# Query and exponentials moved to a PSUM bank, and the projected query to the feed-forward output's bank, in a graph attention kernel

## What is computed

```python
# layers 0 and 1, l = 0, 1 (h = relu(layernorm(x)) @ w_in + b_in at first)
xn = layernorm(h, ln1_g[l], ln1_b[l])
q, k, v = xn @ wq[l] + bq[l], xn @ wk[l] + bk[l], xn @ wv[l] + bv[l]
scores = einsum('ehd,ehd->eh', q[dst], k[src]) * scale
ex = exp(scores - segment_max(scores, dst)[dst])
attn = ex / segment_sum(ex, dst)[dst]
agg = segment_sum(attn * v[src], dst)
h = h + agg @ wo[l] + bo[l]
h = h + gelu(layernorm(h, ln2_g[l], ln2_b[l]) @ w1[l] + b1[l]) @ w2[l] + b2[l]
# layer 2, after x = x + h and h = relu(layernorm(x)): keys K[src] + 0.2 * rel_w[edge_type],
# no feed-forward part; x = x + layernorm(agg @ Wo + bo + h) * gamma + beta
```

## Time and profile before

| | |
|---|---|
| median of 3 runs | 5768.97 us (5768.95 to 5776.74) |
| the profiled execution: its own time | 5769.38 us |
| its span | 5767.4 us, 100749 instructions |
| mean granted clock of TensorE, share of full speed | 0.81 |
| PE busy | 3774.7 us (65%) |
| DVE busy | 3920.1 us (68%) |
| ACT busy | 1907.6 us (33%) |
| POOL busy | 3630.9 us (63%) |
| layer 0, layer 1, layer 2 begin on DVE at | 926.5, 2490.6, 4061.9 us |

### The profile page before, as it was taken

How to read it: one execution, slowest core, us unless ns; L and a number is a source line. 1 busy time by engine, 2 the same in 40 slices (tenths; PEclk the granted TensorE clock), 3 DMA queues, 4 the chain that set the end, 5 groups by cost and what they waited for, 6 DMA issues and landing times. The chain is left out here.

```text
span 5767.4 us, 100749 instructions
## 1 busy us (share of the span) xinstructions
PE 3774.7 (65%) x17126; PEld 2738.3 (47%) x17127; DVE 3920.1 (68%) x6783; ACT 1907.6 (33%) x4023; POOL 3630.9 (63%) x3068
## 2 busy tenths in 40 slices
PE   2056663677778888836777787878456665555555
PEld 2023332455556666525555565656344444444443
DVE  9533333777777777547777777765588888777766
ACT  5023331233334444413333344444222333232333
POOL 0422225788887776457888877753588777666643
PEclk9987776888889999968888899999666666666666
DMA  5022224566556655346666666553455555454442
GB/s 182 1 67 93 93 93 129 164 188 185 180 174 211 199 181 178 109 141 180 197 194 184 191 208 195 181 166 108 128 167 170 161 154 151 143 149 129 132 116 70
DMA packets 361804, 870.94 MB, mean 151 GB/s; under 512 B 142032, under 2 KB 154813, under 8 KB 361748
## 3 DMA queue, kind: packets, MB, share of 16 engines
q0 software_dynamic: 243088, 718.69, 42.4%
q1 hardware_dynamic: 111604, 119.56, 6.5%
q10 hardware_dynamic: 7056, 32.12, 1.4%
HBM read 791.89 MB, written 149.65 MB: 163 GB/s over the span
## 5 line engine op out<-in xcount | busy, mean ns | idle before, releaser
L1036 POOL DMA_INDIRECT kv<-kv_dram,idx x2616 | 3177.7, 1215 | 1232.0 <-issue 753.2
L1492 PE MATMUL ps_acc<-kv,ident 128*128 x5232 | 1430.0, 441 | 206.8 <-DVE kv L1176 205.6
L1492 PEld LDWEIGHTS ps_acc<-kv,ident 128*128 128x128 f32 x5232 | 1168.6, 227 | 491.2 <-issue 287.6
L1098 DVE TENSOR_TENSOR kv<-kv,rec_in (+1 forms) x654 | 790.1, 1220 | 379.4 <-DMA kv<-kv_dram,idx 243.1
L1103 DVE TENSOR_REDUCE sc<-kv 128x32 f32 (+2 forms) x654 | 785.7, 1211 | 13.6 <-DVE kv L1098 12.9
L1176 DVE TENSOR_TENSOR kv<-kv,ex x654 | 756.9, 1220 | 22.1 <-issue 10.6
L1486 PE MATMUL ps_acc<-acc_scaled,ident 128*128 128x256 f32 x306 | 145.9, 569 | 690.9 <-DVE zrun L1168 690.9
L1337 ACT COPY acc<-ps_acc 128x256 f32<-128x256 f32 x153 | 57.0, 372 | 1504.1 <-PE ps_acc L1495 1504.1
L1540 PE MATMUL ps_big<-xnaT,w_ffn 128*128 128x128 f32 x3136 | 376.4, 278 | 135.3 <-ACT xnaT L1394 135.3
L1540 PEld LDWEIGHTS ps_big<-xnaT,w_ffn 128*128 128x128 f32 x3136 | 359.1, 192 | 157.5 <-ACT xnaT L1394 80.1
L1486 PEld LDWEIGHTS ps_acc<-acc_scaled,ident 128*128 128x128 f32 x306 | 60.5, 247 | 743.9 <-DVE zrun L1168 743.9
(11 more groups left out here) (207 smaller groups left out, 5182.9 us busy)
## 6 DMA issues: line engine op xcount, KB each, us to landing
rec_in<-rec_dram SPq DMA_DIRECT2D x147, 512.0 KB, 4.8
rec_dram<-rec_out POOLq DMA_DIRECT2D x98, 512.0 KB, 3.3
kv<-kv_dram,idx POOLq DMA_INDIRECT x2616, 3.8
rec_dram<-rec_in ACTq DMA_DIRECT2D x49, 640.0 KB
windows<-kv SPq DMA_DIRECT2D x46, 408.0 KB, 2.6
rec_in<-rec_dram SPq DMA_DIRECT2D x49, 128.0 KB, 5.4
w_ffn<-in_L_gnn_w SPq DMA_DIRECT2D x4, 1024.0 KB, 6.5
meta<-slot_meta SPq DMA_DIRECT2D x153, 24.0 KB, 3.1
```

Source lines behind the costliest of these rows:

```text
L1036: pool.indirect_dma_start(kv[:, u * W + slot, :], None, kv_dram[l], bass.IndirectOffsetOnAxis(ap=idx[:, u, slot:slot + 1], axis=0), bounds ...
L1098: nc.vector.tensor_tensor(at, at, q, ALU.mult).then_inc(s["mul"], 1)
L1492: mm = nc.tensor.matmul(ps_acc[:, 0:D], ident[:], at[:, :, slot, :].rearrange("p a d -> p (a d)"), start=False, stop=False, skip_group_che ...
```

## The change

The SBUF tile `ex` is gone. The bank `ps_q` now belongs to ACT and DVE alone: its columns 0 to 255 (`ps_query`) hold the query of the block being scored, columns 256 on (`exw`) the exponentials. ACT copies the query from `rec_in` to `ps_query` (`query_row`), for block b+1 within the exp of block b's last round, between the wait for `to_exp` and the exp itself; DVE's `start` waits for this copy (`query`) instead of the record's load. DVE's products read `ps_query`, its weightings and `rescale` read `exw`.

The projected query of a finished block, which had been in `ps_q`, goes to columns 0 to 255 of `ps_w`, whose other half holds the feed-forward output. PE makes it in a step of its own (`next_q`), behind the earlier rounds and after DVE has read the feed-forward output of block b-2 (`second`), and `feed_out` waits for the record of the block before to be copied out (`recq`). In layer 2 the transposed types, the pairs and the products use `ps_kv` and `ps_w` without `ps_q`; the third group of pairs waits for ACT's first `away`. ACT's last block is written out apart from its loop in all layers.

```diff
@@ -182,7 +182,6 @@
-        ex = sb("ex", [P, (W + 1) * 8])
@@ -216,9 +215,10 @@
-        ps_types = ps_q[0:W, 0:P // 2].bitcast(BF16)
-        ps_pairs = [ps_w[:], ps_q[:], ps_kv]
-        ps_rel = [ps_big[:, 0, :], ps_big[:, 1, :], ps_w[:]]
+        ps_query = ps_q[:, 0:D]
+        ps_types = ps_kv[0:W, 0:P // 2].bitcast(BF16)
+        ps_pairs = [ps_w[:], ps_kv, ps_w[:]]
+        ps_rel = [ps_big[:, 0, :], ps_big[:, 1, :], ps_kv]
@@ -597,10 +597,13 @@
-        def project_qkv(l, ofT, done):
-
-            project(ps_kv, ofT, w_qkv[l], B_QKV + 3 * l * D, (0, 2 * D))
-            project(ps_q[:, 0:D], ofT, w_qkv[l], B_QKV + 3 * l * D, (2 * D, 3 * D)).then_inc(done, 1)
+        def project_kv(l, ofT):
+
+            return project(ps_kv, ofT, w_qkv[l], B_QKV + 3 * l * D, (0, 2 * D))
+
+        def project_q(to, l, ofT):
+
+            return project(to, ofT, w_qkv[l], B_QKV + 3 * l * D, (2 * D, 3 * D))
@@ -911,7 +915,7 @@
-            exw = ex[:, 0:(W + 1) * H]
+            exw = ps_q[:, D:D + (W + 1) * H]
@@ -1074,7 +1077,7 @@
-                        q = flat(rec_in[:, one(b % RING), AT_Q:AT_Q + D]).unsqueeze(1).broadcast_to([P, CH, D])
+                        q = ps_query.unsqueeze(1).broadcast_to([P, CH, D])
@@ -1179,7 +1182,8 @@
-                        dve.wait_ge(s["rec"], by_rec * (b + 1))
+                        dve.wait_ge(s["query"], b + 1)
+                        settle(dve)
@@ -1187,7 +1191,7 @@
-                            step(nc.vector.tensor_tensor(prod[:], flat(r[:, :, AT_Q:AT_Q + D]), flat(r[:, :, AT_K:AT_K + D]), ALU.mult))
+                            step(nc.vector.tensor_tensor(prod[:], flat(r[:, :, AT_K:AT_K + D]), ps_query, ALU.mult))
@@ -1345,8 +1349,16 @@
-                    def exp_round(k):
+                    def query_row(b):
+                        act.wait_ge(s["rec"], by_rec * (b + 1))
+                        settle(act)
+                        nc.scalar.copy(ps_query, flat(rec_in[:, one(b % RING), AT_Q:AT_Q + D])).then_inc(s["query"], 1)
+
+                    def exp_round(k, upcoming=None):
                         act.wait_ge(s["to_exp"], k + 1)
+                        if upcoming is not None:
+                            settle(act)
+                            query_row(upcoming)
                         nc.scalar.activation(exw, smw, ACT.Exp, scale=scale).then_inc(s["exped"], 1)
@@ -1434,7 +1446,7 @@
-                        nc.scalar.copy(flat(to[:, :, 2 * D:3 * D]), ps_q[:, 0:D]).then_inc(s["recq"], 1)
+                        nc.scalar.copy(flat(to[:, :, 2 * D:3 * D]), ps_w[:, 0:D]).then_inc(s["recq"], 1)
@@ -1458,7 +1470,7 @@
-                            exp_round(k)
+                            exp_round(k, None if last_block(b) else b + 1)
@@ -1477,7 +1489,8 @@
-                    iterate(act, iteration)
+                    query_row(0)
+                    iterate(act, iteration, whole=NB - 1)
@@ -1497,12 +1510,15 @@
+                        if not isinstance(k, int):
+                            pe.wait_ge(s["relrow"], GROUPS * k)
+                            settle(pe)
                         pe.wait_ge(s["types"], k + 1)
                         nc.tensor.transpose(ps_types, types[:], ident_b[:]).then_inc(s["typesT"], 1)
-                        if not isinstance(k, int):
-                            pe.wait_ge(s["relrow"], GROUPS * k)
                         pe.wait_ge(s["typesTs"], k + 1)
                         for g in range(GROUPS):
+                            if g == 2:
+                                pe.wait_ge(s["away"], k * GROUPS + 1)
@@ -1544,6 +1560,9 @@
                         to = ps_w[:, D:2 * D]
+                        if not isinstance(b, int) or b >= 2:
+                            pe.wait_ge(s["recq"], b - 1)
+                            settle(pe)
                         bias(to, B_2 + l * D)
@@ -1554,12 +1573,18 @@
-                    def next_qkv(b):
+                    def next_kv(b):
...
-                        project_qkv(l + 1, xnbT, s["qkv"])
+                        project_kv(l + 1, xnbT)
+
+                    def next_q(b):
+                        if not isinstance(b, int) or b + 1 < NB:
+                            pe.wait_ge(s["second"], 2 * b + 3)
+                            settle(pe)
+                        project_q(ps_w[:, 0:D], l + 1, xnbT).then_inc(s["qkv"], 1)
@@ -1590,6 +1615,9 @@
+                        if exists(b - 3) and not typed:
+                            next_q(b - 3)
+                        if exists(b):
                             sums(k, chunk0, filled)
```

More of the change, by code:

```diff
@@ L874, in iteration @@
                             settle(pe)
-                        project_qkv(0, xnbT, p_qkv)
+                        project_kv(0, xnbT)
+                        project_q(ps_q[:, 0:D], 0, xnbT).then_inc(p_qkv, 1)
                 iteration(0)
@@ L894, in build @@
             "norm", "residual", "second", "scale1", "scale2", "aggT", "aggTs", "w", "var1", "sd1", "var2", "sd2", "rs1", "xn1", "xT1", "xTs1", "f1", "g", "f2", "rs2", "xn2", "xT2", "xTs2", "qkv", "recq", "types", "typesT", "typesTs", "pairs", "away", "onehot", "relp", "relrow", "outx", "mixed", "last",
-            "used", "taken")}
+            "used", "taken", "query")}
         numbers = sorted(handle.num for handle in between.values())
@@ L920, in last_round, with iterate @@
                 return (round_number(rounds_before + earlier), chunks_before + earlier * CPS, last)
-            def iterate(eng, iteration, peeled=DEPTH):
-                whole = NB - 1 if typed else NB
+            def iterate(eng, iteration, peeled=DEPTH, whole=NB - 1 if typed else NB):
                 for b in range(peeled):
@@ L1580, in iteration @@
                         if exists(b - 3) and not typed:
-                            next_qkv(b - 3)
+                            next_kv(b - 3)
                         if exists(b):
```

## The result

The changed kernel takes 5797.8 us (median of 6 runs, 5795.6 to 5799.1) beside 5773.7 us for the kernel before (6 runs, 5769.0 to 5786.9): the ratio is 1.0038, 95% interval 1.0026 to 1.0051. It is slower by 0.4%, where 5748 us was forecast. That lies inside the stated range of 5700 to 5805 us, but on the other side of the kernel before. The profiled execution has a span of 5795.9 us, 28.5 more than before.

A forecast was written before the change was run, and what follows sets the result against it. POOL was taken to bound blocks of five, DVE and its waits blocks of four. Gains of 44, 19, 26 and 24 us against costs of 83 and 9 gave -21, so 5748 us from 5769.4; range 5700 to 5805.

The forecast's parts named there:

- What bounds the kernel: Layers 0 and 1: POOL bounds blocks of five; DVE and its feed-forward waits, 1.2 and 1.1 us, bound blocks of four.
- The gathers: POOL: DVE operations with two SBUF operands hold gathers; with one operand in PSUM each takes 1.00 us plus 0.30 issue.
- PSUM operands on VectorE at nothing: DVE products and weightings: a PSUM operand leaves durations unchanged; bounds -4 and +4 ns on 1767 instructions, 7 us either way.
- ScalarE's order: Table load and copy now follow L1156: exp ends 2.25 us behind it instead of 0.40, 1.6 us more per block.
- a drain of the same size: Behind ScalarE's table load, by the skill page: 1.4 us more per block, the kernel some 120 us later than the sum.
- blocks of four, three and two, both layers: 52 ..., x 1.6: +83: Layers 0 and 1: 52 blocks with a successor to copy a query for each pay 1.6 us, +83 us.
- The clock: Third-engine rival, blocks of five and six: TensorE's clock or later-landing gathers set the pace; 5793 us, chance 0.17.
- met and free: DVE's wait for `query`, replacing that for `rec`, is met since the load is issued a block ahead; no cost.
- The range: The forecast's own range, 5713 to 5783 us: exp delay -22 and +31, PSUM operand 7, early blocks 10.
- Hidden load: Rival on ScalarE: the chip starts the table load ahead of the wait, 0.3 instead of 1.6 us a block; 5637 us, chance 0.08.
- Layer 2: +11 us for exp behind the copy, -2 in its first blocks' gather waits: +9 us.

The follow-up runs named there:

- e3: The changed kernel with the query read from the record in SBUF again, no copy; only the exponentials in PSUM: 5647.2 us, ratio 0.9779.
- e8: The changed kernel with one exp of a single column, result unused, ahead of both waits so the table loads early: 5666.6 us, ratio 0.9824.
- e6: The changed kernel with spare matmuls in TensorE's idle time ahead of the sums, layers 0 and 1: 5755.5 us, ratio 0.9964.
- e5: The kernel before with a second wait between `to_exp` and exp, so the table load comes late; no operand moved: 5880.6 us, ratio 1.0183.
- e7: The kernel before with TensorE's part of the change alone (bank and place of the query's projection, their waits): 5775.0 us, ratio 1.0005.
- e10: The changed kernel with the next query's copy behind the block's last weighting and exp behind `to_exp` alone: 5571.9 us, ratio 0.9655.
- e1: The changed kernel with ScalarE's wait for the record ahead of the wait for `to_exp`: 5761.5 us, ratio 0.9975.
- e4: The changed kernel with the exponentials in SBUF again; only the query in PSUM, copied as there: 5802.9 us, ratio 1.0060.
- e9: The changed kernel with both e8's early exp table load and e6's spare matmuls: 5650.9 us, ratio 0.9792.
- e16: The kernel before with the spare matmuls of e6 and nothing else, third try: 5768.9 us, ratio 0.9992.
- e17: e5 (kernel before, late table load) with the spare matmuls of e6, third try: 5827.4 us, ratio 1.0084.

## Why the prediction was wrong

- **What bounds the kernel**: right for blocks of five, which take 30.7 and 31.4 us (30.4 and 31.2 forecast) with no wait for a gather left on DVE. For blocks of four it said that the feed-forward output "hangs in turn on DVE's `agg`". That held for 8 of 18 blocks, with 9.7 us of waiting for `agg` in all. A second chain, from the end of the sums through PE's own queue, was as long within about half a microsecond.
- **The gathers**: right. 1.006 us in blocks of five against the forecast's 1.00, and none over 1.26 in layers 0 and 1. A held gather ended 0.87 us behind the operation that held it in e3 (the prediction estimated 0.96). The inference of the Trainium skill ("SBUF — State Buffer", Who interferes with whom), that `tensor_tensor` does not hold up descriptor generation, is contradicted by e3: 1.89 us beside a product with two SBUF operands, 1.00 beside a weighting with one in PSUM.
- **PSUM operands on VectorE at nothing**: right, 1215 and 1216 ns.
- **ScalarE's order**: right in its mechanism and close in size. Exp ends 2.35 us behind L1159 against 2.25, and L1167 and L578 wait 1.7 us more, not 1.6. The load is 1.28 us; and taking it out of the path in some 94 blocks (x 1.28 = 120 us) brought back 124 to 131 us in e8, which leaves no room for a drain of the same size.
- **The step that failed** is the term "blocks of four, three and two, both layers: 52 ..., x 1.6: +83". It counted the delay of exp itself and let everything behind it shift by the same amount. But a delay on DVE ahead of the sums is idle time on PE, and the sums that follow it ran more of their time at the lower of the two clock levels: 1.4 us longer per block in the mean of layer 0. Of that, 9.7/18 = 0.5 us is covered by the slack against `agg`, and most of the rest shows as DVE's longer wait at L1256, 0.7 us. The term was +117. Of the 34 us that it missed, spare matmuls (e6) give back 22: the stretches of 522.8, 220.9, 532.7 and 226.5 us take 513.7, 215.4, 526.0 and 225.8. The clock was among the rivals, but put into blocks of five and six, where L1256 waits only 5.4 us in 15 blocks; it acted where PE's output is on the path.
- **The start of a block** is part of the other 12 us. The idle time ahead of L1193 is put down to "issue". In the 18 blocks of four of layer 0 it is 41.7 to 42.4 us in e3, e5 and e7, where VectorE waits for the record there, 43.3 in e10, where the wait for `query` stands later, and 46.6 to 48.9 in the changed kernel, e1, e4, e6 and e8, where it waits for `query` there. So it goes with DVE's new wait, which the prediction called met and free; how a wait that is met costs 0.3 us stays open.
- **The range**: the prediction's own range for its forecast, 5713 to 5783, does not follow from the bounds that it names. Added up they give 5748 - 39 = 5709 and 5748 + 48 = 5796.
- **Hidden load**: the rival's 5637 us against e8's 5666.6. It charged 0.3 us a block; in e8 the wait at L578's place (L579 there) is 8.6/18 = 0.48 us, and L1256's place waits 27.0/18 = 1.5 us in blocks of four of layer 0, which is the clock again (19.4/18 = 1.1 with spare matmuls, e9):

```profile
L1257 DVE TENSOR_TENSOR rec_out<-h,ps_w 128x256 f32 x18 | 7.6, 421 | 27.0 <-PE ps_w L1573 27.0
...
L579 DVE RECIPROCAL rs<-sd 128x1 f32<-128x1 f32 x36 | 5.7, 159 | 8.6 <-ACT sd L575 8.6
```

- **Layer 2**: +7 from its first gather to the end beside the forecast's +9, but this is luck. From DVE's first instruction on it took 5795.9 - 4089.5 = 1706.4 us, 0.9 more than before; the other 6 lie at its start, where VectorE now waits for the first query's copy, which ScalarE makes behind the first relation rows. The prediction did not name this wait. Some 4 us more lie between layers 1 and 2, and 2 us ahead of layer 0.

```profile
4089.50 0.07 DVE L1190 MEMSET mrun<- 128x8 f32 x1 [29.72 <-ACT ps_q L1355]
```
```profile
4061.91 0.07 DVE L1186 MEMSET mrun<- 128x8 f32 x1 [24.00 <-DMA rec_in<-rec_dram]
```

## What to carry to other kernels

An added wait ahead of an instruction can cost more than itself: it decides what is done while the engine waits anyway, here a table load of 1.28 us. Look at the order of the compiled program, down to the register work that may take the wait over. And a delay on one engine is idle time on the next: before you let a chain "shift by the same amount", see whether TensorE's granted clock falls behind the gap, and which second chain is nearly as long. When an edit should win and does not, look for the wait that took its place, as the gathers did in e16. When two operands do the same kind of good, try each alone: one of them gave 2.2% with nothing added on ScalarE, the other carried the whole price, until its copy was moved to where its engine waits anyway.

## What the runs showed of the hardware

- Spare matmuls in idle time made a kernel faster, by 0.7% (e6) and 0.9% (e17). In the first, two gaps of about 2 us ahead of the sums went with a granted clock of 0.89 over the blocks of four of layer 0, and filling them brought it to 0.99.
- A gather that meets a VectorE operation with two SBUF operands ends 0.87 us behind that operation (e3); beside one with a PSUM operand it takes 1.00 us.
- The sum over the exponentials (`L1168`, now `L1171`; 128x200, strided by head) takes 366 ns from PSUM and 508 from SBUF:

```profile
L1171 DVE TENSOR_REDUCE zrun<-ps_q 128x8 f32<-128x200 f32 x18 | 6.6, 366 | 0.6
```
```profile
L1168 DVE TENSOR_REDUCE zrun<-ex 128x8 f32<-128x200 f32 x18 | 9.1, 508 | 0.6
```

- exp writes PSUM in 0.33 us where it took 0.37 into SBUF.
